# Fourth layer's attention heads on one core: two score tiles per round, three banks for turned rows, one result bank

## What is computed

```python
q = _ln(qkv[:, :, 0].transpose(0, 2, 1, 3), qn_g, qn_b)
k = _ln(qkv[:, :, 1].transpose(0, 2, 1, 3), kn_g, kn_b)
v = qkv[:, :, 2].transpose(0, 2, 1, 3)
scores = jnp.einsum('bhnd,bhmd->bhnm', q, k) / jnp.sqrt(jnp.float32(HD))
attn = jax.nn.softmax(scores, axis=-1)
o = jnp.einsum('bhnm,bhmd->bhnd', attn, v)
```

## Time and profile before

| | us |
|---|---|
| median of 3 runs | 2008.98 (2007.1 to 2012.11) |
| span of the profiled execution | 2000.0 |
| the stage of the heads, first score to last PV | 1107.7 to 1734.1, 626 |
| PE busy over the whole span | 1818.6 (91%) |
| DVE, ACT, POOL busy | 1480.6, 1182.2, 813.1 |
| mean granted clock of PE | 0.937 |

### The profile page before, as it was taken

How to read it: one execution, slowest core, us unless ns; L and a number is a source line. 1 busy time by engine, 2 the same in 40 slices (tenths; PEclk the granted TensorE clock), 3 DMA queues, 4 the chain that set the end, 5 groups by cost and what they waited for, 6 DMA issues and landing times. The chain is left out here.

```text
span 2000.0 us, 37648 instructions
## 1 busy us (share of the span) xinstructions
PE 1818.6 (91%) x14478; PEld 1176.4 (59%) x14478; DVE 1480.6 (74%) x2537; ACT 1182.2 (59%) x2031; POOL 813.1 (41%) x736
## 2 busy tenths in 40 slices
PE   7998999899799989998998799999999999892886
PEld 5766699797333333346766455555555555582786
DVE  6676646647789899986887777777777777537796
ACT  3333233424177778875666777777777777523563
POOL 3464710554312120012666445544444444205576
PEclk9999999899589899999999899999999999995888
DMA  5000000202513112104669554454544555115452
GB/s 156 1 24 4 14 1 1 64 1 97 167 41 92 39 39 58 47 29 138 217 213 290 142 123 110 103 127 95 119 114 120 146 120 135 59 51 171 151 158 48
DMA packets 196195, 191.30 MB, mean 96 GB/s; under 512 B 64496, under 2 KB 154352, under 8 KB 195760
## 3 DMA queue, kind: packets, MB, share of 16 engines
q1 hardware_dynamic: 192944, 184.69, 34.1%
q0 software_dynamic: 3072, 4.20, 1.2%
HBM read 121.20 MB, written 67.37 MB: 94 GB/s over the span
## 5 line engine op out<-in xcount | busy, mean ns | idle before, releaser
L1601 POOL TENSOR_SCALAR l3h_prob<-l3h_prob,l3h_inv 128x1024 f32<-128x1024 f32 x256 | 287.1, 1121 | 322.5 <-DVE l3h_inv L1573 322.5
L1567 DVE TENSOR_REDUCE l3h_nmax<-l3h_score 128x1 f32<-128x1024 f32 x256 | 313.4, 1224 | 139.1 <-PE l3h_score L1510 139.0
L1801 DVE TENSOR_REDUCE l2h_nm<-l2h_rowb 128x1 f32<-128x1024 f32 x256 | 303.2, 1218 | 40.6 <-PE l2h_rowb L1733 40.1
L1851 ACT ACTIVATE l2h_pT<-l2h_score 128x512 f32<-128x512 f32 x512 | 273.8, 598 | 67.9 <-PE l2h_score L1749 49.7
L1591 ACT ACTIVATE l3h_prob<-l3h_score,l3h_nmax 128x1024 f32<-128x1024 f32 x256 | 285.8, 1116 | 37.7 <-DVE l3h_nmax L1567 2.7
L1533 PE MATMUL l3h_out<-l3h_pT,l3h_vs 128*64 128x512 f32 x1024 | 274.4, 617 | 0.0
L1559 ACT ACTIVATE l3h_pT<-l3h_ring 128x512 f32<-128x512 f32 x256 | 152.8, 597 | 106.4 <-PE l3h_ring L1521 105.9
L1521 PEld LDWEIGHTS l3h_ring<-ident,l3h_prob 64*128 64x128 f32 x4096 | 173.0, 138 | 35.5 <-issue 7.8
L1557 DVE COPY l3h_pT<-l3h_ring 128x512 f32<-128x512 f32 x256 | 172.0, 672 | 2.0 <-PE l3h_ring L1521 1.9
L1521 PE MATMUL l3h_ring<-ident,l3h_prob 64*128 64x64 f32 x4096 | 169.4, 222 | 2.2 <-DVE l3h_pT L1557 1.9
L1763 PE MATMUL l2h_out<-l2h_pT,l2h_vs 128*32 128x256 f32 (+1 forms) x1792 | 164.8, 443 | 0.0
(11 more groups left out here) (481 smaller groups left out, 4346.2 us busy)
## 6 DMA issues: line engine op xcount, KB each, us to landing
q3first<-l_q SPq DMA_DIRECT2D x64, 256.0 KB, 4.8
l3h_Q<-l_q SPq DMA_DIRECT2D x64, 256.0 KB, 4.9
l_q<-l3qkv_hi SPq DMA_DIRECT2D x16, 512.0 KB, 5.1
l_q<-l3qkv_lo SPq DMA_DIRECT2D x16, 512.0 KB, 4.5
l_k<-l3qkv_hi SPq DMA_DIRECT2D x16, 512.0 KB, 4.5
l_k<-l3qkv_lo SPq DMA_DIRECT2D x16, 512.0 KB, 3.3
k3first<-l_k SPq DMA_DIRECT2D x64, 128.0 KB, 5.0
l3h_vs<-l_v SPq DMA_DIRECT2D x32, 256.0 KB, 3.2
```

The source lines that it names most:

```text
L1567: dve.tensor_reduce(self.nmax[:, t % 4:t % 4 + 1], self.score[t % 2][:, :], AX.X, ALU.max, negate=True).then_inc(self.maxes, 1)
L1601: pool.tensor_scalar(self.prob[:, q, :], self.prob[:, q, :], self.inv[:, q:q + 1], self.vscale, ALU.mult, ALU.mult).then_inc(self.scaled, 1)
L1801: dve.tensor_reduce(self.nm[:, mr % 2, at:at + 1], self.rowb[h][:, :], AX.X, ALU.max, negate=True).then_inc(self.maxes, 1)
L1851: act.activation(self.pT[:, g % 4, h, c * C:(c + 1) * C], self.score[v % 3][:, :], ACT.Exp).then_inc(self.exps, 1)
```

## The change

Engines take two tiles (g and g + 1, g even) per round:

- PE: turns of g - 4, scores of g and of g + 1, turns of g - 3, PV of g - 12 and of g - 11. LAG goes from 3 to 4.
- The turned rows go round three banks, `ring[(2 g + half) % 3]`, so the turns of g wait for DVE's copy of g - 2 and ACT's of g - 1 (before: both of g - 1). The bank comes from one of the two result banks; the first PV of a head now waits for ACT's copy of the head before it.
- DVE and ACT change halves: ACT empties half 0, DVE half 1.
- DVE: copy of g - 4, maximum of g, one reciprocal of 128 x 2 for g - 2 and g - 1, maximum of g + 1, copy of g - 3.
- ACT: copy of g - 4, every fourth round the copy of a result, copy of g - 3, exponents of g and of g + 1.
- POOL scales one tile at a time as before; SP's loop isn't touched.

```diff
-    LAG = 3
+    LAG = 4
...
-        self.ring = [s.ps(f"ring{i}") for i in range(2)]
-        self.ob = [s.ps(f"out{i}") for i in range(2)]
+        self.ring = [s.ps(f"ring{i}") for i in range(3)]
+        self.ob = s.ps("out")
...
         def turn(g):
+            if not 0 <= g < TB * self.N:
+                return
             pe.wait_ge(self.scaled, g + 1)
-            self.need(pe, self.emptied_d, g)
+            self.need(pe, self.emptied_d, g - 1)
             self.need(pe, self.emptied_a, g)
...
-                self.need(pe, self.ocopied, n - 1)
+                self.need(pe, self.ocopied, n)
...
-        for g in range(TB * self.N + self.LAG + TB):
+        for g in range(0, TB * self.N + self.LAG + TB, 2):
+            turn(g - self.LAG)
             if g < TB * self.N:
                 score(g)
-            gt = g - self.LAG
-            if 0 <= gt < TB * self.N:
-                turn(gt)
-            n, kk = divmod(gt - TB, TB)
+                score(g + 1)
+            turn(g + 1 - self.LAG)
+            n, kk = divmod(g - self.LAG - TB, TB)
             if n >= 0:
                 mix(n, kk)
+                mix(n, kk + 1)
+
+    def turn_bank(self, g, half):
+        return self.ring[(2 * g + half) % 3]
...
+        def inverses(g):
+            q = g % 4
+            dve.wait_ge(self.exps, g + 2)
+            self.need(dve, self.scaled, g - 2)
+            dve.reciprocal(self.inv[:, q:q + 2], self.total[:, q:q + 2]).then_inc(self.invs, 1)
+
+        for g in range(0, TB * self.N + self.LAG, 2):
+            self.empty(dve, g - self.LAG, 1)
             if g < TB * self.N:
...
+                maximum(g)
+            if 2 <= g <= TB * self.N:
+                inverses(g - 2)
+            if g < TB * self.N:
+                maximum(g + 1)
+            self.empty(dve, g + 1 - self.LAG, 1)
...
+        for g in range(0, TB * self.N + self.LAG + TB + 2, 2):
+            self.empty(act, g - self.LAG, 0)
+            n, k = divmod(g - self.LAG - 2 * TB, TB)
+            if n >= 0 and k == 0:
+                ocopy(n)
+            self.empty(act, g + 1 - self.LAG, 0)
             if g < TB * self.N:
...
+                exponents(g)
+                exponents(g + 1)
...
-            pool.wait_ge(self.invs, g + 1)
+            pool.wait_ge(self.invs, g // 2 + 1)
```

More of the change, by code:

```diff
@@ L1520, in turn @@
                     r = slice(half * P // 2, (half + 1) * P // 2)
-                    mm = pe.transpose(self.ring[half][:, kk * P // 2:(kk + 1) * P // 2],
+                    mm = pe.transpose(self.turn_bank(g, half)[:, kk * P // 2:(kk + 1) * P // 2],
                                       self.prob[r, g % 4, kk * P:(kk + 1) * P], self.ident[r, r])
@@ L1530, in mix @@
                 pe.wait_ge(self.vloaded[n % 2], 16 * (n // 2 + 1))
-                self.need(pe, self.ocopied, n - 1)
+                self.need(pe, self.ocopied, n)
             for c in range(2):
-                mm = pe.matmul(self.ob[n % 2][c * self.hd:(c + 1) * self.hd, :], self.vs[:, n % 2, kk, :],
+                mm = pe.matmul(self.ob[c * self.hd:(c + 1) * self.hd, :], self.vs[:, n % 2, kk, :],
                                self.pT[:, n % 2, kk, c * C:(c + 1) * C], start=kk == 0, stop=kk == TB - 1)
@@ L1554, in empty @@
         dst = self.pT[:, n % 2, :, at:at + P // 2]
-        src = self.ring[half][:, :].rearrange("p (k q) -> p k q", k=TB)
-        if half == 0:
+        src = self.turn_bank(g, half)[:, :].rearrange("p (k q) -> p k q", k=TB)
+        if half == 1:
             eng.tensor_copy(dst, src).then_inc(self.emptied_d, 1)
@@ L1561, in dve_program, with maximum @@
     def dve_program(self, dve):
-        for g in range(TB * self.N + self.LAG):
-            if g < TB * self.N:
[L1564 to L1575, removed]
+        def maximum(g):
+            dve.wait_ge(self.scores, g + 1)
+            self.need(dve, self.exps, g - 3)
+            dve.tensor_reduce(self.nmax[:, g % 4:g % 4 + 1], self.score[g % 2][:, :], AX.X, ALU.max,
+                              negate=True).then_inc(self.maxes, 1)
+        def inverses(g):
[5 more added lines that the diff above has]
+            self.empty(dve, g - self.LAG, 1)
+            if g < TB * self.N:
+                maximum(g)
[4 more added lines that the diff above has]
+            self.empty(dve, g + 1 - self.LAG, 1)
     def act_program(self, act):
@@ L1580, in ocopy, with exponents @@
             self.need(act, self.stored[n % 2], 32 * (n // 2))
[L1581 to L1585, removed]
-            if g < TB * self.N:
[L1587 to L1595, removed]
+            act.activation(self.osb[:, n % 2, :], self.ob[:, :], ACT.Copy).then_inc(self.ocopied, 1)
+        def exponents(g):
+            q = g % 4
+            act.wait_ge(self.maxes, g + 1)
+            self.need(act, self.turned, 2 * (g - 3))
+            self.need(act, self.invs, g // 2 - 1)
+            act.activation(self.prob[:, q, :], self.score[g % 2][:, :], ACT.Exp, bias=self.nmax[:, q:q + 1],
+                           accum_out=self.total[:, q:q + 1]).then_inc(self.exps, 1)
+        for g in range(0, TB * self.N + self.LAG + TB + 2, 2):
[4 more added lines that the diff above has]
+            self.empty(act, g + 1 - self.LAG, 0)
+            if g < TB * self.N:
+                exponents(g)
+                exponents(g + 1)
     def pool_program(self, pool):
```

## The result

Four runs of the changed kernel took 2040.1 us in the median (2033.6 to 2048.9), those of the kernel before 2008.0 (1997.4 to 2012.1). The ratio is 1.017, with a 95% interval of 1.0126 to 1.0213: slower by 32 us. The forecast was 2036, in a range of 2010 to 2056. The profiled execution has a span of 2036.5 us against 2000.0.

The account below looks back on a forecast made before the run. PE's order was taken as the bound, one tile every 2.39 us for 19 heads, with loads just in time. Span 2000.0 + 15 (late loads, start, end) + 12 (clock) = 2027, plus 9 to the median: 2036, range 2010 to 2056.

Parts of the forecast that it names:

- PE's round: Two tiles on PE, turns, scores, turns, PV: 4.42 us per round, 17.7 per head against 19.17.
- DVE, ACT, POOL at nothing: Work of the other engines per round, DVE 3.93 and ACT 3.8 us, fits in 4.42; copies and scalings cost nothing.
- The chain through ACT: Turns, ACT's copy, two exponents, scores, next turns: 4.4 us, equal to PE's sum, costing nothing to 0.2 per round.
- The loads decide: Q and K loads queued behind load_v come late: PE needs them in 9.3 us, against 11.9 before, and waits.
- The way to `load_v`: From a head's first scores to the next load_v: 8.45 us, against 7.3 before.
- Heads 2 to 20, +4: Ordinary heads, reckoned as 3 to 21: 19.38 us each against 19.17, 19 times, +4 us.
- L: Time from load_v to the last landing of the eight loads: 10.9 us in the mean, 12.57 behind o3T; nothing shortens it.
- Heads 21 to 28, +9, and 29 and 30, -1: Heads behind o3T loads, reckoned as 22 to 29: 21.06 us against 19.90, +9; heads 30 and 31: 18.6 against 19.2, -1.
- The clock, +12: PE's clock falls to half speed after 3.3 us waits behind o3T: 8 x 0.9 x 1.7 = +12 us.
- Start and end, +2 and +1: Start: chain through ACT gives 4.4 per pair of tiles against 3.8, +2; end: paired turns wait for ACT's copy, +1.
- The sum for the stage, +27: All terms of the stage together: +15 us for late loads, start and end, and +12 for the clock.
- The 9 us between span and median: Allowance of 9 us added to the forecast span of 2027 to give the median, 2036.

Follow-up runs that it names:

- the first experiment: The changed kernel with SP's loop reordered: V's load for head n after the Q and K loads of n + 1, before the store; 1964.99 us, 0.9764 of the kernel before.
- the three variants of order and banks: Changed kernel, load_v(n) after load(n + 1): second turns between the scores, 2009.24 us; between the PV, 2094.06 us; two turned-row and two result banks, 1989.88 us.

## Why the prediction was right, point by point

- **PE's round.** Forecast 4.42 from 0.58 + 1.39 + 0.58 + 1.87, measured 4.45 from 0.52 + 1.47 + 0.58 + 1.87. Two steps are off by 0.06 and 0.08 and cancel, by luck: behind the turns it is 0.52, at the lower bound of the earlier trace rows, and from the first tile's scores to the second's it is 0.77, since the first pair behind the turns takes 0.31; from the second tile's scores to the turns it is the 0.70 of three pairs. Weight loads did go on beside matmuls on the same rows: behind that first pair, five more follow at 0.23 each, as the earlier trace rows let expect. That goes against the rule cited in the prediction from the Trainium skill, page TensorE: Matmul & The Clock Gate, Part 3 (The mechanism), though the same section names a background weight buffer as a second way to load ahead.
- **DVE, ACT, POOL at nothing.** Held in the settled rounds, as the first experiment shows with the loads out of the way. The chain through ACT is a near limit (4.4 against 4.45), and the three variants of order and banks ran into it or into a copy. POOL was not free in heads 5 to 8, as that experiment also shows, and at the end the single result bank cost 0.79, which I had called free.
- **The loads decide.** Held, and shown by the first experiment: the same kernel with loads on time is 75 us faster than the changed one by their medians. The way to `load_v` was forecast 8.45 and is 8.50.
- **Heads 2 to 20, +4.** Measured +1.1. L is 10.67 in the mean and not 10.9: 19 x 0.23 = 4.4 less, and the longer way gives 1.0 back. "Nothing shortens L" was the step that was off; with `load_v` held in the old order L stayed at 10.9, so the shorter burst belongs to the new order, but what in it does that was not tried.
- **Heads 21 to 28, +9, and 29 and 30, -1.** Measured +8.5 and +0.9 without the clock. For the last two I took an L of 10.1 from before; it is 10.7 and 11.4.
- **The clock, +12.** Measured +15.8, and with the clock kept up by added matmuls heads 22 to 29 took 164.9 us instead of 180.7. It fell in eight heads of eight, and in three of them stayed down for two stretches of 3.4 us instead of one. The count was right; the price per fall, 1.7, lies between the two that occurred, 1.5 and 2.7.
- **Start and end, +2 and +1.** Measured +1.7 and +1.8.
- **The sum for the stage, +27.** Measured +29.7, with terms that are off by more than the sum: heads 2 to 20 by -3, the clock by +4, heads 29 and 30 by +2. That it is off by 3 only is in part luck; that late loads and the clock behind `o3T` decide is not.
- **The 9 us between span and median.** Wrong as it was put. The profiled execution after took 2038.21 us for a span of 2036.5, so 1.7 lies around the span; the rest of the 9 was that the profiled execution before was a quick one (one run of the kernel before with a span of 2000.0 took 2001.77 us, 7 under the median). In the ten traces of this study the 266 to 274 us behind the stage, the same code in all, vary by 8 us, and before is the lowest. The number 2036 rests on the stage's +27 against +29.7 measured, and on this allowance, which helped for a reason that I had not given; that is luck too.

Why the traces of single executions differ behind the stage (clock 0.83 before, 0.81 after there) stays open.

## What to carry to other kernels

When an order on the bound engine is changed, follow every release that hangs on a moved instruction through the queues to its next use: here the PV that releases a burst of loads came 1.2 us later in the head while PE reached the scores that need them 2.6 us sooner behind it (9.3 instead of 11.9), and the gain of 1.4 us per head turned into waiting. Before giving such a change up, see whether the burst must stand behind that wait at all; with that wait one head earlier, the loads came 10 us early, and the two edits together were worth 2.4%, 0.5% of it without the new order. And where a wait of some 2 us or more stands in a dense stretch of PE, look whether the clock falls behind it: the wait may cost 1.5 us more than its length.

## What the runs showed of the hardware

- The granted clock fell behind waits of some 2 us already. Counted as the delay of the first scores, between 2.06 and 2.5 us both happened: 2.06 (head 27 where `o3T` came later), 2.2 (head 31 of the changed kernel) and 2.5 (head 25 of the kernel with `load_v` held) passed at full clock; 2.13 (head 31 where `o3T` came later) and 2.4 (head 28 of the changed kernel) were followed by a fall. All of 2.8 us and more without added work were, among them the seven others of the changed kernel (2.9 to 4.3). Its ordinary delays, up to 1.8 us, passed.
- Where PE's work was less dense, shorter waits were enough. In the kernel with the second turns between the two scores, at the start of the stage, the clock fell twice, behind waits of 1.23 and 1.17 us that followed others of 1.33 and 1.42. The first of the two, the turns, and the granted clock (last but two) from there on:

```profile
1120.67 1.11 PE L1523 MATMUL l3h_ring<-ident,l3h_prob 64*128 64x64 f32 x16 [1.23 <-ACT l3h_pT L1568]
```

```profile
1120.70:1124.10 3.40, 3.40 (x40) 3.19 (x42) 1.39 (x3) 1.69 (x3) 2.22 (x2) 0.50 0.02 5
```

- A fall lasted one stretch of 3.4 us or two, in the middle of dense work, and cost 1.4 to 1.6 or 2.6 to 2.8 us. Twenty-two matmuls put into the wait, 2.8 us of work followed by up to 1.33 idle, avoided it in all eight heads.
- A switch from scores to PV costs more (0.90 from one to the other, for three pairs that take 0.77 when turns follow) than from turns to PV (0.58, for turns that take 0.52 when scores follow).
